# Layer-norm statistics taken tile by tile in the stage ahead, in a two-layer decoder kernel

## The reference, cut to what matters

```python
def _layernorm(x, axis=-1, eps=1e-05):
    m = jnp.mean(x, axis=axis, keepdims=True)
    v = jnp.var(x, axis=axis, keepdims=True)
    return (x - m) / jnp.sqrt(v + eps)

x = x + _L0_attn_ref(_layernorm(x, axis=-1), ...)     # gated delta net
x = x + _L0_xattn_ref(_layernorm(x, axis=-1), ...)    # masked cross attention
x = x + _L0_ffn_ref(_layernorm(x, axis=-1), ...)      # ternary MLP
x = x + _L1_attn_ref(_layernorm(x, axis=-1), ...)     # selective scan, then a wave equation
x = x + _L1_xattn_ref(_layernorm(x, axis=-1), ...)    # cross attention
x = x + _L1_ffn_ref(_layernorm(x, axis=-1), ...)      # experts
```

## Time and profile before

| what | value |
|---|---|
| median of 3 runs | 5511.79 us |
| lowest and highest | 5505.73 and 5520.55 us |
| the profiled execution's own time | 5518.12 us |
| its span, first to last instruction | 5516.0 us |
| PE busy, share of the span | 89% |
| DVE busy | 54% |
| ACT busy | 40% |
| POOL busy | 20% |
| mean granted TensorE clock | 0.950 of full speed |

### The profile page before, as it was taken

How to read it: one execution, slowest core, us unless ns; L and a number is a source line. 1 busy time by engine, 2 the same in 40 slices (tenths; PEclk the granted TensorE clock), 3 DMA queues, 4 the chain that set the end, 5 groups by cost and what they waited for, 6 DMA issues and landing times. The chain is left out here.

```text
span 5516.0 us, 87839 instructions
## 1 busy us (share of the span) xinstructions
PE 4904.1 (89%) x37194; PEld 2801.5 (51%) x37194; DVE 2994.9 (54%) x5866; ACT 2192.0 (40%) x3522; POOL 1084.4 (20%) x671
## 2 busy tenths in 40 slices
PE   6979996999999999999899997477737999999897
PEld 3468884666666666666544443133323333333465
DVE  5767773555555555555400004599966666766350
ACT  5734342444444444344211112455512544445421
POOL 0145553011011011000000000388840000000021
PEclk9989997999999999999999998699978999999898
DMA  2221111000000000000200001000001000000123
GB/s 88 103 90 53 49 46 42 7 10 19 16 7 21 13 10 7 21 7 7 85 0 0 0 0 59 38 16 23 16 5 39 1 13 1 13 1 1 56 80 106
DMA packets 47691, 160.98 MB, mean 29 GB/s; under 512 B 7184, under 2 KB 19024, under 8 KB 38496
## 3 DMA queue, kind: packets, MB, share of 16 engines
q1 hardware_dynamic: 45776, 151.33, 7.7%
q0 software_dynamic: 1536, 4.20, 0.2%
HBM read 111.08 MB, written 44.43 MB: 28 GB/s over the span
## 5 line engine op out<-in xcount | busy, mean ns | idle before, releaser
L1480 DVE CUSTOM_DVE_ANT_0 ma_prob<-ma_ring,ma_mask 128x400 f32<-128x400 f32 (+1 forms) x1024 | 527.4, 572 | 260.6 <-PE ma_ring L1584 260.6
L1932 DVE TENSOR_REDUCE fa_part<-fa_ring 128x1 f32<-128x512 f32 x768 | 486.6, 681 | 222.0 <-PE fa_ring L2053 203.1
L1879 ACT ACTIVATE fa_prob<-fa_ring 128x512 f32<-128x512 f32 (+1 forms) x832 | 441.6, 598 | 406.3 <-PE fa_ring L2053 328.4
L2053 PE MATMUL fa_ring<-fa_K,fa_Q 32*128 32x512 f32 (+1 forms) x2048 | 530.7, 546 | 2.0
L1493 DVE COPY ma_PT<-ma_ring 128x512 f32<-128x512 f32 x512 | 341.9, 689 | 287.4 <-PE ma_ring L1594 287.1
L1594 PE MATMUL ma_ring<-ident,ma_prob 128*128 128x128 f32 (+1 forms) x3328 | 462.3, 280 | 6.7 <-ACT ma_prob L1439 6.7
L2073 PE MATMUL fa_ring<-fa_Qm,fa_K 32*128 32x512 f32 (+1 forms) x1664 | 457.7, 629 | 2.3 <-DVE fa_Qm L1949 2.3
L1608 PE MATMUL ma_pv<-ma_PT,ma_V 128*64 128x256 f32 (+1 forms) x3328 | 457.8, 393 | 0.0
L1406 POOL TENSOR_SCALAR ma_diag<-ident,ma_rtotal 128x128 f32<-128x128 f32 x256 | 149.7, 602 | 1533.6 <-DVE ma_rtotal L1498 1533.6
L2267 PE MATMUL ffn_mid<-ffn_hid,ffn_h 128*128 128x512 f32 x1024 | 441.5, 593 | 9.7 <-DVE ffn_hid L2233 6.3
L1594 PEld LDWEIGHTS ma_ring<-ident,ma_prob 128*128 128x128 f32 (+1 forms) x3328 | 357.1, 141 | 163.6 <-issue 105.1
(11 more groups left out here) (386 smaller groups left out, 7882.7 us busy)
## 6 DMA issues: line engine op xcount, KB each, us to landing
gd_rows<-gp_tile SPq DMA_DIRECT2D x16, 1024.0 KB, 4.2
gd_c_vg<-gd_rows SPq DMA_DIRECT2D x16, 1024.0 KB
moe_w<-in_moe_w SPq DMA_DIRECT2D x16, 1024.0 KB, 7.3
ma_w<-in_ma_w SPq DMA_DIRECT2D x32, 384.0 KB, 3.1
gd_rows<-gp_gate SPq DMA_DIRECT2D x16, 512.0 KB, 5.1
gd_c_qk<-gd_rows SPq DMA_DIRECT2D x16, 512.0 KB
ffn_h<-in_ffn_h SPq DMA_DIRECT2D x2, 4096.0 KB, 22.7
ma_ctxT<-in_ctxT SPq DMA_DIRECT2D x4, 1601.0 KB, 6.8
```

The lines of the kernel that those rows point to most:

```text
L1480: nc.vector.tensor_tensor_reduce(prob[:, u % 2, t, h, k0:k0 + width], bank("S", u, t, n, h)[:, 0:width], mask[:, b % 2, half * 2 + t, k0:k ...
L1879: nc.scalar.activation(prob[0:n, (u * KT + kt) % PROBS, j, :], bank("scores", u, kt, j)[0:n, :], ACT.Exp, scale=SCALE).then_inc(p_ready, 1)
L1932: ins = nc.vector.tensor_reduce(part[:, u % 2, t, j, n:n + 1], src[:], AX, ALU.max)
L2053: last = nc.tensor.matmul(bank("chunk", u, i)[:, at * w:(at + 1) * w], Q[rows, b % 2, g, tile * P:(tile + 1) * P], K[rows, b % 2, g, k0:k0 ...
```

## The change

A tile `row_stats` of 16 x 6 values is held for the whole program as `c.stats`. Where `x` gets its last sum in a stage, VectorE now waits for its own addition and then takes `bn_stats` of the tile or the two tiles that it has just written. The norm of the next stage is called with `counted=True` and begins with `bn_aggr`. Five norms change so: those of ma, ffn, the first of the selective scan, fa and moe. The norm of gd, ahead of all, and the second one of the selective scan stay as they were.

```diff
-def layernorm(nc, c, name, src, dst, gain=None, shift=None, keep=None):
+def layernorm(nc, c, name, src, dst, gain=None, shift=None, keep=None, counted=False):
...
-        stats = s.sb("stats", [P, NT, 6])
+        stats = c.stats if counted else s.sb("stats", [P, NT, 6])
...
             chain = Chain(dve, vec)
-            for t in range(NT):
-                last = nc.vector.bn_stats(stats[:, t, :], src[:, t, :])
-            chain.link(last)
+            if not counted:
+                for t in range(NT):
+                    last = nc.vector.bn_stats(stats[:, t, :], src[:, t, :])
+                chain.link(last)
...
                 nc.vector.tensor_tensor(rows, rows, bank("out", g, b)[:, 0, 0:D], ALU.add).then_inc(dve_taken, 1)
+                dve.wait_ge(dve_taken, nth["out", g, b])
+                nc.vector.bn_stats(c.stats[:, b * TB + g, :], rows)
...
                 nc.vector.tensor_tensor(rows, rows, bank("out", b, t)[:, 0:D], ALU.add).then_inc(dve_taken, 1)
+                dve.wait_ge(dve_taken, nth["out", b, t])
+                nc.vector.bn_stats(c.stats[:, b * TB + t, :], rows)
...
                 nc.vector.tensor_tensor(rows, rows, bank("out", b, half)[:].rearrange("p (t d) -> p t d", d=D), ALU.add
                                         ).then_inc(ring_free, 1)
+                dve.wait_ge(ring_free, nth["out", b, half])
+                for t in range(2):
+                    nc.vector.bn_stats(c.stats[:, b * TB + half * 2 + t, :], rows[:, t, :])
...
                     nc.vector.tensor_tensor(row, row, scaled[:, t % 2, :], ALU.add).then_inc(added, 1)
+                    dve.wait_ge(added, i * NT4 + (t + 1))
+                    nc.vector.bn_stats(c.stats[:, ds(i * NT4 + t, 1), :].rearrange("p a d -> p (a d)"), row)
...
-        layernorm(nc, c, "ss_ln0", c.x, None, keep=xa)
+        layernorm(nc, c, "ss_ln0", c.x, None, keep=xa, counted=True)
...
                     nc.vector.tensor_tensor(rows, rows, out_ps[b % 2][h][:], ALU.add).then_inc(added, 1)
+                    dve.wait_ge(added, 2 * b + h + 1)
+                    for t in range(2):
+                        nc.vector.bn_stats(c.stats[:, TB * b + 2 * h + t, :], rows[:, t, :])
...
+        c.stats = stack.enter_context(nc.sbuf_tensor("row_stats", [P, NT, 6], F32))
```

More of the change, by code:

```diff
@@ L1271, in _ @@
                 sp.dma_start(w[:, 1], c.dram["ma_w"][1]).then_inc(w_loaded[1], 16)
-        layernorm(nc, c, "ma_ln", c.x, c.xnT)
+        layernorm(nc, c, "ma_ln", c.x, c.xnT, counted=True)
         wide = s.sb("wide", [P, MP, P])
@@ L1733, in _ @@
                 sp.dma_start(ctxT[:], c.dram["ctxT"][0]).then_inc(ctx_loaded, 16)
-        layernorm(nc, c, "fa_ln", c.x, c.xnT)
+        layernorm(nc, c, "fa_ln", c.x, c.xnT, counted=True)
         bv_wide = s.sb("bv_wide", [P, FG, P])
@@ L2189, in _ @@
                     sp.dma_start(w[n][:], c.dram[f"ffn_{n}"]).then_inc(loaded[n], 16)
-        layernorm(nc, c, "ffn_ln", c.x, c.xnT)
+        layernorm(nc, c, "ffn_ln", c.x, c.xnT, counted=True)
         gate = s.sb("gate", [P, 2, 512])
@@ L3125, in _ @@
                 nc.gpsimd.memset(zeros[:], 0.0).then_inc(zeros_ready, 1)
-        layernorm(nc, c, "moe_ln", c.x, c.xnT, keep=xn)
+        layernorm(nc, c, "moe_ln", c.x, c.xnT, keep=xn, counted=True)
         logits = s.sb("logits", [P, NT, NE])
```

## The result

The changed kernel took 5481.3 us, the median of four executions (5480.06 to 5482.77), against 5510.7 us before; the ratio is 0.9946, with a 95% interval of 0.9933 to 0.9958. I had forecast 5492.5 us and a range of 5482 to 5508. So the kernel is faster, as forecast, but the gain was 29.4 us and not some 19, and the median lies 0.7 us under the range.

The account below looks back on a forecast made before the run. Between barriers at the stage seams, the norm on VectorE was taken as the bound. 26.8 - 0.2 - 0.3 - 2.24 - 0.9 - 3.9 = 19.3 us; 5511.8 - 19.3 = 5492.5 us, range 5482 to 5508.

Parts of the forecast that it names:

- loads or clock take the saving back: Behind norms: ma's mask load or a lower TensorE clock takes 1 to 5 us; time 5493 to 5498; chance 0.14.
- The removed statistics: In five norms, the stretch from first bn_stats to first bn_aggr goes: 5.36 us each, 26.8 us together.
- table load: In four norms ScalarE's table load now ends last, delaying the root some 0.05 us each; 0.2 us lost.
- The mask: At ma's start, POOL's first work would wait for the mask's load: 0.3 us lost, bounds 0 and 0.6.
- The tails: At stage ends, wait plus last statistics add 0.45 us in gd and ma, 0.56 in ffn, 0.78 in fa.
- The cover in gd, ma and ffn: Inside these stages VectorE's idle time hides the statistics, cost nothing; rival of cover failing partly or wholly: chance 0.15.
- fa's 0.9 us: Inside fa, a reduction freeing a ring bank starts 0.3 us late three times: 0.9 us, bounds 0 and 0.9.
- The wave part's 3.9 us: VectorE's queue is the path: first batch 1.3 us, second 1.6, end 1.0 including the last statistics; 3.9 together.
- held by POOL: POOL's work delays statistics: 7.5 us inside gd, about 2 in the wave part; time 5502; chance 0.08.
- The wait: VectorE's wait for its own addition takes 0.04 us, or 0.15 with a loop register's target; dear-wait rival: chance 0.03.

Follow-up runs that it names:

- the block levelled: Two more 512-column products in each of 16 steps of the scan stage's first block: changed kernel 5514.98 us, kernel before 5536.01 us.
- its distance back: Changed kernel with thirteen more unread bn_stats at the head of the selective scan's second norm; 5495.73 us, ratio 0.9977 to the kernel before.
- a longer norm: Kernel before with ten more unread bn_stats at the head of the selective scan's second norm; 5511.0 us, ratio 1.0007.
- the statistics taken twice: Changed kernel's statistics inside the stages, but all five norms take and use their own again; 5521.33 us, ratio 1.0022 to the kernel before.
- fa's norm alone: Kernel before with statistics moved in the wave part alone, so only fa's norm is shortened; 5504.61 us, ratio 0.999.

## Why the prediction came out as it did

**The mechanism was right.** Five norms lose their statistics, and with the block levelled the change is worth 21.0 us where the sum said 19.3; the two profiles of the changed kernel say 17.5 and 22.4. That the sum came so close is luck in part: of the terms below some were 0.4 to 0.7 us too good and others 0.9 to 1.3 too bad.

**The step that failed is the rival "loads or clock take the saving back", with its size: "The clock may fall either way, so 3 us stand on both sides."** The clock isn't worth 3 us here but up to 20, from execution to execution, in one block that the change doesn't touch: with a granted clock of 0.69 to 0.78 over it, it took 181.9 to 161.6 us. The place was foreseen ("TensorE's first products behind a norm"), the size and the direction were not. I had taken the mean clock of 0.95 and the runs below full speed behind the norms, and not looked at which stretch makes the runs differ, though three runs of one kernel lay 15 us apart. The range ought to have reached lower: four quick executions, 29.4 us under before, of which some 20 are the change and the rest the clock, were enough to leave it. By how little it was missed is chance as well; the five later executions have their median at 5488.5, inside.

**Is the shorter block the change's doing, in part?** The block took 161.6, 164.9 and 168.4 us in the three profiles of kernels with all five norms shortened and nothing put back, and 178.5 to 181.9 in three of four that run the old code up to there unaltered, 170.0 in the fourth. The nine executions' gain of 24.8 us is also 2.8 more than the levelled 22.0, mean against mean, but the two differences together are uncertain by about 2.3. And giving the changed kernel its distance back cost 7 to 14 us for a pause of 4.2. Against a fixed effect stand 170.0 us with a longer norm and 178.5 with the statistics taken twice. It may be that the change moves the odds of a good clock; these runs don't settle it. It would take some ten profiles of each kernel.

The terms, one by one:

**The removed statistics** gave, with all that changed up to the next main block, 5.36 us in ma and 5.14, 4.75, 5.30 and 5.12 in the others (first profile). The four with a table load gave 0.06 to 0.61 us less than ma's, where I had 0.05 for each; the 4.75 is 5.13 in the norm itself and 0.38 lost again in the second norm behind it, in every kernel with the short one. Right in sum, to 0.6 us.

**The mask** costs nothing in the first profile and 0.7 us in the second, where SP's last issue was short and the norm early. There POOL starts 12.09 us behind the `bn_aggr` (at 881.37) and not 11.38, released by the DMA as I had feared (timeline):

```profile
893.47 8.61 POOL L1401 TENSOR_SCALAR ma_mask<-ma_mask 128x1604 bf16<-128x1604 uint8 x2 [37.30 <-DMA ma_mask<-in_ma_mask]
```

In the other profiles with ma's norm shortened POOL isn't released by the DMA. So 0.3, with bounds of 0 and 0.6, was a fair term.

**The tails** were right at 3.0, which is what the second profile has. The 4.0 of the first contains 1.05 us in one DMA issue (1.65 against 0.60 us), which in the second profile takes 0.53:

```profile
880.40 0.53 SPq L1274 DMA_DIRECT2D ma_w<-in_ma_w  x1
```

**The cover in gd, ma and ffn** holds as far as can be seen. The fourth tile of gd's iteration 6 keeps 0.28 us of the 0.74 before it, where I had worked out 0.37 (timeline):

```profile
536.46 0.42 DVE L993 TENSOR_TENSOR x<-x,gd_c_ring 128x256 f32<-128x256 f32 x1 [2.40 <-PE gd_c_ring L1164]
536.91 0.43 DVE L995 BATCH_NORM_STATS2 row_stats<-x 128x6 f32<-128x256 f32 x1
537.62 0.69 DVE L926 TENSOR_TENSOR gd_c_TT<-gd_c_XT,gd_c_lev 128x512 f32<-128x512 f32 x1 [0.28 <-PE gd_c_lev L1071]
```

ffn's main block was 623.3 us in one profile and 621.6 in the other, where it was 621.6 before; the 1.7 us are TensorE's time for the same 1536 matmuls (609.5 against 607.8), and the kernel before with ten more `bn_stats` has 1.4 of them too, without a statistic in ffn. In gd and ma a cost of 1 to 2 us would not be seen: their main blocks scatter by 5.8 and 2.3 us over the seven profiles with the old code there. With the statistics, gd's is 1.6 us shorter on the mean of six profiles and ma's 1.4 longer.

**fa's 0.9 us** was the wrong end of my bounds. The timeline of the second pair, counterpart of the earlier trace rows:

```profile
4573.30 0.69 DVE L1978 TENSOR_TENSOR x<-x,fa_ring 128x512 f32<-128x512 f32 x1 [1.98 <-PE fa_ring L2111]
4574.02 0.75 DVE L1982 BATCH_NORM_STATS2 row_stats<-x 128x6 f32<-128x256 f32 x2
4574.69 1.27 DVE L1937 TENSOR_REDUCE fa_part<-fa_ring 128x1 f32<-128x512 f32 x2
4576.44 0.69 DVE L1937 TENSOR_REDUCE fa_part<-fa_ring 128x1 f32<-128x512 f32 x1 [0.48 <-PE fa_ring L2081]
```

The reduction starts 1.39 us after the addition and not 1.09, 0.30 late as I said. But the one behind it starts 3.14 us after the addition, and before it was 3.15 (4611.14 - 4607.99): its idle time shrank from 0.77 to 0.48, and TensorE lost nothing. I had followed the delay one instruction too few. Nor are the 0.7 us that fa's block gained the statistics' doing: the kernel in which only fa's norm is short, with nothing added in fa, has 0.6 of them. The row of before:

```profile
4611.14 0.69 DVE L1932 TENSOR_REDUCE fa_part<-fa_ring 128x1 f32<-128x512 f32 x1 [0.77 <-PE fa_ring L2073]
```

**The wave part's 3.9 us** (with its tail) were 2.6. The second batch cost 1.57 us as forecast and the last two additions nearly nothing (0.04 for 0.2). The first batch failed: 0.22 for 1.3 (timeline; before: the earlier trace rows).

```profile
4096.61 0.68 DVE L3056 TENSOR_TENSOR x<-x,wave_out 128x512 f32<-128x512 f32 x1
4097.33 0.75 DVE L3059 BATCH_NORM_STATS2 row_stats<-x 128x6 f32<-128x256 f32 x2
...
4099.38 1.52 DVE L3020 TENSOR_SCALAR wave_turns<-wave_up 128x1024 f32<-128x1024 f32 x1
4100.93 1.42 DVE L3021 TENSOR_SCALAR wave_turns<-wave_turns 128x1024 f32<-128x1024 f32 x1
...
4109.10 1.22 DVE L3027 TENSOR_TENSOR wave_s<-wave_up 128x1024 f32<-128x1024 f32 x1
...
4118.75 0.68 DVE L3056 TENSOR_TENSOR x<-x,wave_out 128x512 f32<-128x512 f32 x1
...
4121.51 1.21 DVE L3038 SCALAR_TENSOR_TENSOR wave_kdv<-wave_d,wave_kdv 128x1024 f32<-128x1024 f32 x1
```

`shape` starts 2.77 us after the addition and not 1.80, 0.97 later, as forecast (1.07). But from its start to line 3027 it takes 9.72 us, where it took 10.47 before (to the row below): it begins 0.92 us behind POOL's first instruction now, where it began 0.04 ahead of it, and so stands beside POOL for less of it. The kernel with fa's norm alone shows both in one trace: 10.47 us for the batch that begins 0.04 ahead and has no statistics before it, 9.72 for the one that begins 0.92 behind.

```profile
4140.07 1.21 DVE L3017 TENSOR_TENSOR wave_s<-wave_up 128x1024 f32<-128x1024 f32 x1
```

**The rival "held by POOL"** is refuted: the statistics keep 0.43 us in gd and in the wave part. **The wait**: between the end of an addition and its statistic lie 0.03 us (877.33 + 0.42 to 877.78). The Trainium skill (VectorE: DVE Perf Modes, The DRAIN you can't avoid) has a semaphore between two VectorE instructions cost nothing extra; with two waits in place of one a batch takes 2.76 us and not 2.64, so here it costs a little.

**Experts** went from 317.9 us to 319.1, and to 315.9 in the second profile. Its first 64 products, at the start of the main block, took 11.66 us before, 13.79 after and 10.75 in the second profile, with a granted clock of 0.59, 0.50 and 0.64 over the first 14 us; between the two profiles of the changed kernel they are 3.0 of the 3.2 us. This is what I had meant by first products behind a norm in a lower clock, and here its size is 1 to 3 us, as I had it (timelines: after, before, after again):

```profile
5159.14 13.79 PE L3454 MATMUL moe_aux<-moe_router,xnT 128*128 128x8 f32 x64 [1.85 <-PEq L50]
```

```profile
5198.13 11.66 PE L3441 MATMUL moe_aux<-moe_router,xnT 128*128 128x8 f32 x64 [1.85 <-PEq L50]
```

```profile
5160.78 10.75 PE L3454 MATMUL moe_aux<-moe_router,xnT 128*128 128x8 f32 x64 [1.85 <-PEq L50]
```

## What to carry to other kernels

Here work between two barriers cost its full length (5.36 us for 16 instructions), and the same work in front of a wait for another engine that was longer than it cost next to nothing: moving 80 instructions of 0.41 us out of five seams was worth some 20 us, read off from the start and the end of a stretch and the idle times of its new places. Follow a delay until an idle time takes it up, and not only to the next instruction. Before giving a range, find the stretch that makes executions of the same kernel differ, by the windows' granted clock in it, and let the range hold its whole swing.

## What the runs showed of the hardware that I had not expected

One block's time was 69.8 us plus TensorE's own, in 13 profiles, and TensorE's time for the same 195 matmuls went from 91.7 to 112.0 us with a granted clock of 0.78 to 0.69. The clock stood at 0.94 to 1.00 in the block's first 30 us, with TensorE busy for 28 to 29 of them; in the third 30 us it was 0.78 in the one profile and 0.96 in the other. What decides between the two, no run here shows. The Trainium skill (TensorE: Matmul & The Clock Gate, Part 1: The HAM clock gate) puts the cost of the clock's warming up at under 1% of a kernel and has the phase vary from run to run; the variation is seen here, though as a fall in the middle of the kernel and not as a warming up, and it stays under 1%: this one block moved by 20.2 us, 0.37% of the kernel. But that is as much as the change itself is worth (21.0 us). Further, VectorE work that begins a little later beside a long POOL instruction can be shorter for it (10.47 to 9.72 us).
